# A state-space layer with a gated feed-forward branch: the gate product in bf16 pieces, the rank columns inside the steps' weights, the scan's masks built during the first steps

## What is computed

```python
x = L0_attn_hidden_states                       # (1, 1024, 512)
xn = _layernorm(x, axis=-1)
x = x + _L0_attn_ref(xn, ...) + _L0_ffn_ref(xn, ...)
```

```python
inter = xf @ c1_w.T @ c2_w.T                    # rank 16, 1792 units
blk = inter.reshape(B * T, n_blocks, SPARSITY)  # blocks of 32 units
idx = jnp.argmax(blk, axis=-1) + jnp.arange(0, INTER, SPARSITY)
h = jax.nn.relu(jnp.einsum('bkm,bm->bk', w1[idx], xf))
out = jnp.einsum('bk,bkm->bm', h, w2t[idx])
```

## Time and profile before

| | us |
|---|---|
| median of three runs | 1941.55 (1940.65 to 1942.32) |
| the profiled execution | 1946.74 |
| its span, first to last instruction | 1945.0 |
| mean granted clock of TensorE | 0.993 |
| prologue, up to the first inward product of the scan's tiles | 258.4 |

### The profile page before, as it was taken

One profiled execution on the slowest core, in us unless ns is written; L12 is line 12 of the kernel. 1 busy time (PEld: TensorE's weight loads), 2 busy tenths in 40 slices (PEclk: granted clock), 3 DMA queues, 4 the chain that ended last, 5 costly groups with the idle time before them and its releaser, 6 DMA issues.

```text
span 1945.0 us, 29309 instructions
## 1 busy us (share of the span) xinstructions
PE 1888.3 (97%) x10416; PEld 1478.3 (76%) x10416; DVE 1454.6 (75%) x1701; ACT 1169.6 (60%) x1908; POOL 951.2 (49%) x693
## 2 busy tenths in 40 slices
PE   7998999999999999999998999999999999999997
PEld 4776777777777777777776777878787878787875
DVE  6876645878787877778785878686878787877766
ACT  3334346767677776767676556566665656565643
POOL 6656643555555455555553444444344444444432
PEclk9999999999999999999999999999999999999998
DMA  2324463455454646464646353333424242424231
GB/s 88 119 82 141 137 218 93 134 164 181 148 188 135 210 131 225 136 213 128 208 131 222 86 153 128 114 110 95 146 77 155 83 161 82 156 77 150 77 115 44
DMA packets 123102, 264.62 MB, mean 136 GB/s; under 512 B 18112, under 2 KB 24384, under 8 KB 122704
## 3 DMA queue, kind: packets, MB, share of 16 engines
q1 hardware_dynamic: 88240, 161.55, 26.4%
q10 hardware_dynamic: 34720, 101.20, 16.2%
HBM read 216.82 MB, written 45.88 MB: 135 GB/s over the span
## 4 chain that ended last, share of the span: by engine, by line
PE 86%; issue 3%; POOL 3%; DVE 3%; DMA 3%; ACT 2%; ACTq 1%; SPq 0%; DVEq 0%; POOLq 0%
PE bank L1065 39%; PE bank L1123 6%; PE bank L1164 6%; PE bank L1185 5%; PE bank L1178 5%; PE bank L1098 5%; PE bank L1085 5%; PE bank L1130 3%; PE bank L721 3%; PE bank L694 3%; PE bank L1110 3%; PE bank L680 1%; DMA wlo_scratch<-stage 1%; POOL wxp L314 1%; DMA ecs<-ecs_scratch 1%
## 5 line engine op out<-in xcount | busy, mean ns | idle before, releaser
L1065 PE MATMUL bank<-xnp,wxp 128*128 128x512 f32 x3432 | 864.8, 404 | 11.3 <-POOL wxp L1443 6.4
L1065 PEld LDWEIGHTS bank<-xnp,wxp 128*128 128x128 f32 x3432 | 636.4, 189 | 164.0 <-POOL wxp L1443 16.6
L1443 POOL TENSOR_TENSOR wxp<-wxs,wxp 128x512 fp32r<-128x512 f32 x286 | 382.8, 1341 | 537.0 <-ACT wxp L1294 536.4
L1543 DVE SCALAR_TENSOR_TENSOR conv<-bank,cws,conv 128x509 f32<-128x509 f32 (+2 forms) x480 | 357.9, 746 | 11.3
L1301 ACT ACTIVATE conv<-bank,cbs,cws 128x512 f32<-128x512 f32 x160 | 124.2, 776 | 281.8 <-PE bank L1065 263.1
L1474 POOL TENSOR_TENSOR yl<-gT,yh 128x1024 fp32r<-128x1024 f32 x63 | 151.8, 2409 | 214.3 <-ACT yh L1359 214.3
L1294 ACT ACTIVATE wxp<-wxs 128x512 fp32r<-128x512 f32 x286 | 178.1, 623 | 0.7 <-DMA wxs<-wp 0.7
L1646 DVE SCALAR_TENSOR_TENSOR M<-M,gb 128x1024 f32<-128x1024 f32 x128 | 171.9, 1344 | 7.5 <-DVE gb L1638 0.5
L1345 ACT ACTIVATE ya<-xT,dch 128x128 f32<-128x128 f32 x512 | 156.1, 390 | 0.0
L1336 ACT ACTIVATE M<-bank 128x1024 f32<-128x1024 f32 x64 | 65.7, 1026 | 137.0 <-PE bank L1130 137.0
L1178 PE MATMUL bank<-wosh,yh 128*128 128x512 f32 x512 | 135.7, 407 | 5.1 <-issue 5.0
(11 more groups left out here) (166 smaller groups left out, 2847.0 us busy)
## 6 DMA issues: line engine op xcount, KB each, us to landing
wxs<-wp SPq DMA_DIRECT2D x288, 256.0 KB, 2.7
wosh<-whi_scratch ACTq DMA_DIRECT2D x64, 512.0 KB, 6.2
wosl<-wlo_scratch ACTq DMA_DIRECT2D x64, 512.0 KB, 11.2
ecs<-ecs_scratch ACTq DMA_DIRECT2D x112, 256.0 KB, 4.4
stage<-wout SPq DMA_DIRECT2D x64, 256.0 KB, 3.0
...
```

What stands on the lines that cost most here:

```text
L1065: last = pe.matmul(bank(k), wxp[:, k % 2, a, kk, :], xnp[:, b, kk, :], start=kk == 0 and a + b == 0, stop=kk == KT - 1 and a == 1)
L1443: pool.tensor_tensor(wxp[:, k % 2, 1], wxs[:, k % AHEAD], wxp[:, k % 2, 0], ALU.subtract).then_inc(w_lo, 1)
L1543: last = dve.scalar_tensor_tensor(out=conv[:, n % CB, back:], in0=bank(k)[:, 0:TH - back], scalar=cws[:, g, j, i:i + 1], in1=conv[:, n % C ...
```

## The change

**The gate product.** Ranks and c2 are each cut into three bf16 pieces that add up to the f32 value. Of the nine products of pieces the eight largest are kept, and the eight pairs stand side by side in the contraction: 8 slots of 16 rows make 128 rows. `tT` and `c2T` hold the pieces so, and `gate` is four bf16 matmuls with 128 rows. POOL cuts c2 (five operations), TensorE turns the 14 blocks (`turn_blocks`), ACT copies them (`blocks`). DVE cuts the ranks (`pack`, six operations per half), TensorE turns them (`turn_ranks`), ACT copies (`ranks`).

**The rank product.** c1's 16 columns are appended to the 128 of W_dt; `steps_of` computes both in 144 columns, and `to_rank` goes. `steps_of(0)` moves ahead of the flips of the second half; the DMA of its weights moves up in SyncE's queue.

**The masks.** Five of POOL's seven operations of the front and the three selects ahead of the loop move into turns 0 to 6 of the loop (`mask_part`), behind the turn's last `low`.

```diff
+SLOTS = P // RANK
...
-        c1s = sb(ctx, "c1s", [P, KT, RANK])
-        c2s = sb(ctx, "c2s", [RANK, INTER])
-        wdts = sb(ctx, "wdts", [P, KT, NH])
+        c2f = sb(ctx, "c2f", [P, FT, RANK])
+        c2p = sb(ctx, "c2p", [P, FT, SLOTS, RANK], BF16)
+        c2T = sb(ctx, "c2T", [P, FT, P], BF16)
+        wdts = sb(ctx, "wdts", [P, KT, NH + RANK])
...
-        tT = sb(ctx, "tT", [RANK, L])
+        rk = sb(ctx, "rk", [P, CH, RANK])
+        rkp = sb(ctx, "rkp", [P, CH, SLOTS, RANK], BF16)
+        tT = sb(ctx, "tT", [P, HALVES, TH], BF16)
...
+        early_blocks = gates.bitcast(BF16)
+        late_blocks = banks[0][:, TH:].bitcast(BF16)
+
+        def strips(half):
+            return banks[1 if half else 2].rearrange("p (c n) -> p c n", c=CH)
...
-            sp.dma_start(c1s[:], c1).then_inc(s_wc, 16)
-            sp.dma_start(c2s[:], c2).then_inc(s_wc, 16)
+            sp.dma_start(c2f[:], c2).then_inc(s_c2, 16)
+            sp.dma_start(wdts[:, :, 0:NH], wdt).then_inc(s_wc, 16)
+            sp.dma_start(wdts[:, :, NH:], c1).then_inc(s_wc, 16)
             sp.dma_start(wxs[:, 0], source(0)).then_inc(d_f[0], 16)
...
-            sp.dma_start(wdts[:], wdt).then_inc(s_wdt, 16)
...
-            pool.wait_ge(s_mask, 2)
-            pool.affine_select(out=segl[:], in_=segl[:], compare_op=ALU.is_ge, fill=0.0, base=0,
-                               pattern=[[0, 2], [0, CH], [1, P]], channel_multiplier=-2).then_inc(s_mask, 1)
...
-            pool.wait_ge(s_mask, 5)
...
+            pool.wait_ge(s_c2, 16)
+            three = c2f[:].unsqueeze(2).broadcast_to([P, FT, 3, RANK])
+            two = c2f[:].unsqueeze(2).broadcast_to([P, FT, 2, RANK])
+            pool.tensor_copy(c2p[:, :, 0::3], three).then_inc(s_cp, 1)
+            pool.wait_ge(s_cp, 1)
+            pool.tensor_tensor(c2f[:], c2f[:], c2p[:, :, 0], ALU.subtract).then_inc(s_cp, 1)
+            pool.wait_ge(s_cp, 2)
+            pool.tensor_copy(c2p[:, :, 1::3], three).then_inc(s_cp, 1)
+            pool.wait_ge(s_cp, 3)
+            pool.tensor_tensor(c2f[:], c2f[:], c2p[:, :, 1], ALU.subtract).then_inc(s_cp, 1)
+            pool.wait_ge(s_cp, 4)
+            pool.tensor_copy(c2p[:, :, 2::3], two).then_inc(s_cp, 1)
+            low(0)
             pool.wait_ge(s_part, 1)
             pool.tensor_tensor(xnp[:, 1], xnz[:], xnp[:, 0], ALU.subtract).then_inc(s_split, 1)
-            low(0)
             low(1)
...
-            for m in range(PARTS):
-                pool.wait_ge(s_mask, 5 + m)
...
+
+            def mask_part(n):
+
+                if n == 0:
+                    pool.wait_ge(s_mask, 2)
+                    pool.affine_select(out=segl[:], in_=segl[:], compare_op=ALU.is_ge, fill=0.0, base=0,
...
+                if n == 1:
+                    pool.affine_select(out=segr[:], in_=segr[:], compare_op=ALU.is_ge, fill=FAR, base=0,
...
+                if n == 2:
+                    pool.wait_ge(s_mask, 4)
+                    pool.affine_select(out=segl[:], in_=segl[:], compare_op=ALU.is_ge, fill=0.0, base=1,
...
+                if n == 3:
+                    pool.wait_ge(s_stage, 1)
+                    pool.wait_ge(s_lo, item1(n + 2) + 1)
+                    pool.memset(segr[PAIRS:], 0.0).then_inc(s_stage, 1)
+                    pool.wait_ge(s_stage, 2)
+                    pool.memset(segl[PAIRS:], 1.0).then_inc(s_mask, 1)
+                    pool.wait_ge(s_mask, 5)
+                if 4 <= n < 4 + PARTS:
+                    m = n - 4
+                    pool.wait_ge(s_mask, 5 + m)
+                    pool.affine_select(out=segr[:], in_=segr[:], compare_op=ALU.not_equal, fill=-1.0,
...
                 if n + 2 < STEPS:
                     low(item1(n + 2))
+                mask_part(n)
...
+                act.wait_ge(s_tt, half + 1)
+                act.activation(tT[:, half], spare.bitcast(BF16), ACT.Copy).then_inc(s_tc, 1)
...
             spread(0)
             for t in range(CH):
                 turned_x(t)
+            high(0)
+            part_x(0)
+            blocks(0)
             spread(1)
-            part_x(0)
+            blocks(1)
+            turned_x(4)
+            turned_x(5)
             ranks(0)
-            high(0)
-            for t in range(CH, NT):
-                turned_x(t)
+            turned_x(6)
+            turned_x(7)
+            high(1)
             part_x(1)
-            ranks(1)
-            high(1)
             copy_mask(0)
...
                 if n == 1:
                     act.wait_ge(s_sp, 2)
                     act.activation(tot[:], tot[:], ACT.Ln).then_inc(s_dact, 1)
+                if n == 1:
+                    ranks(1)
...
-                dve.tensor_tensor(v[:, half * CH:(half + 1) * CH, :],
-                                  banks[2][:, half * 512:(half + 1) * 512].rearrange("p (t h) -> p t h", t=CH),
+                dve.tensor_tensor(v[:, half * CH:(half + 1) * CH, :], strips(half)[:, :, 0:NH],
...
+            def pack(half):
+
+                dve.wait_ge(s_dtm, half + 1)
+                dve.tensor_copy(rk[:], strips(half)[:, :, NH:NH + RANK]).then_inc(s_tp, 1)
+                dve.wait_ge(s_tp, 6 * half + 1)
+                if half:
+                    dve.wait_ge(s_tt, half)
+                dve.tensor_copy(rkp[:, :, 0:3], rk[:].unsqueeze(2).broadcast_to([P, CH, 3, RANK])).then_inc(s_tp, 1)
+                dve.wait_ge(s_tp, 6 * half + 2)
+                dve.tensor_tensor(rk[:], rk[:], rkp[:, :, 0], ALU.subtract).then_inc(s_tp, 1)
+                dve.wait_ge(s_tp, 6 * half + 3)
+                dve.tensor_copy(rkp[:, :, 3:6], rk[:].unsqueeze(2).broadcast_to([P, CH, 3, RANK])).then_inc(s_tp, 1)
+                dve.wait_ge(s_tp, 6 * half + 4)
+                dve.tensor_tensor(rk[:], rk[:], rkp[:, :, 3], ALU.subtract).then_inc(s_tp, 1)
+                dve.wait_ge(s_tp, 6 * half + 5)
+                dve.tensor_copy(rkp[:, :, 6:8], rk[:].unsqueeze(2).broadcast_to([P, CH, 2, RANK])).then_inc(s_tp, 1)
...
-            for t in range(CH, NT):
-                normalize(t)
+            normalize(4)
+            normalize(5)
+            pack(0)
+            normalize(6)
+            normalize(7)
...
                     add_bias(1)
+                    pack(1)
...
@@ -675,9 +741,11 @@
                 half, f = n // FT, n % FT
                 if n:
                     pe.wait_ge(s_m, 4 * n - 2)
+                if f == 0:
+                    pe.wait_ge(s_tc, half + 1)
+                    pe.wait_ge(s_cc, 2)
                 for c in range(CH):
-                    t = half * CH + c
-                    last = pe.matmul(gates[:, c * P:(c + 1) * P], tT[:, t * P:(t + 1) * P], c2s[:, f * P:(f + 1) * P],
+                    last = pe.matmul(gates[:, c * P:(c + 1) * P], tT[:, half, c * P:(c + 1) * P], c2T[:, f, :],
...
+                if n == 3:
+                    pe.wait_ge(s_tc, 2)
...
-            def to_rank(half):
+            def steps_of(half):
                 pe.wait_ge(s_xnT, CH * (half + 1))
-                for k in range(KT):
-                    last = pe.matmul(banks[3][0:RANK, half * TH:(half + 1) * TH], c1s[:, k, :],
-                                     (xn1 if half else xnz)[:, k, :], start=k == 0, stop=k == KT - 1)
-                last.then_inc(s_r, 1)
-
...
-            def steps_of(half):
                 for c in range(CH):
-                    t = half * CH + c
                     for k in range(KT):
-                        last = pe.matmul(banks[2][:, t * P:(t + 1) * P], normed(t)[:, k, :], wdts[:, k, :],
+                        last = pe.matmul(strips(half)[:, c, 0:NH + RANK], normed(half * CH + c)[:, k, :], wdts[:, k, :],
...
+            def turn_blocks():
+                pe.wait_ge(s_const, 6)
+                pe.wait_ge(s_cp, 5)
+                for f in range(FT):
...
+                    last = pe.transpose(target, c2p[:, f].rearrange("p s r -> p (s r)"), identb[:])
+                    if f in (SLOTS - 1, FT - 1):
+                        last.then_inc(s_ct, 1)
...
+            def turn_ranks(half):
+                pe.wait_ge(s_tp, 6 * (half + 1))
+                for c in range(CH):
+                    last = pe.transpose(spare.bitcast(BF16)[:, c * P:(c + 1) * P],
+                                        rkp[:, c].rearrange("p s r -> p (s r)"), identb[:])
+                last.then_inc(s_tt, 1)
+
             for t in range(CH):
                 flip(t)
+            turn_blocks()
             pe.wait_ge(s_wc, 32)
-            to_rank(0)
+            steps_of(0)
             flip(4)
             flip(5)
-            pe.wait_ge(s_const, 6)
-            pe.wait_ge(s_rc, 1)
-            gate(0)
+            turn_ranks(0)
             flip(6)
             flip(7)
-            to_rank(1)
+            gate(0)
             inward(0)
             gate(1)
-            pe.wait_ge(s_rc, 2)
             turn(0)
-            pe.wait_ge(s_wdt, 48)
-            steps_of(0)
...
                     pe.wait_ge(s_v, 2)
```

(6 more changed lines are left out.)

39 lines of the change are left out of this document (19 added, 20 removed).

## The result

The changed kernel takes 1949.23 us (median of 11 runs, 1945.84 to 1951.59), the kernel before 1943.18 us in the same comparison (11 runs): ratio 1.0029, 95% interval 1.0021 to 1.0038. It is slower by some 6 us; 1925.5 was forecast. The profiled execution took 1948.32 us, span 1946.6, mean granted clock 0.988.

What follows compares the result with a forecast made beforehand. TensorE was taken as the prologue's bound, except the store loop in steps 13 to 19. Terms -7.2, -2.1, -3.4, -0.4 and -2.9 summed to -16.0 us: 1930.7, less 5.2 for the median, 1925.5; range 1919 to 1933.

Steps and rivals of the forecast that it cites:

- front: Prologue up to step 1: outward product 0 starts at 40.2 instead of 47.41 us, step 1 at 43.2; -7.2 us.
- steps 1 to 8: Shorter gates minus waits for POOL and mutual delay: -2.1 us, ends -6.9 and +1 (DVE's 7 us steps rule).
- rival C: Steps 13 to 19: idle gaps lower TensorE's clock; +3, 1928.5 us, chance 0.13; falls in all seven steps: 8.4, 1933.5.
- steps 20 to 27: Six gates give -5.2, but POOL's casts and subtractions of csT in steps 21 to 23 stand in the way; -2.9 us.
- rival E: All gates: a bf16 gate with 128 rows takes as long as before; -5.2, 1936.4 us; chance 0.05.
- DVE's five pick operations take 3.22 ... so the mask stands at 30.2: Front, after gate 0: the picks keep their profiled 3.22 us, so the mask is ready at 30.2 us.
- Eight gates: -6.9: Steps 1 to 8: each of eight gates saves 0.86 us where TensorE is the bound; -6.9 us.
- 11.5 + m: Steps 1 to 8: POOL's us for two steps with mask part m, against 2 x 6.33 for TensorE; excess +3.1 us.
- +0.8 for mutual delay: Steps 1 to 8: DVE and POOL delaying each other through the moved mask parts costs 0.8 us for all.
- A: Masks and picks fill POOL and DVE; steps 1 to 8 gain nothing; -11.9, 1929.6 us; chance 0.18.
- D: Steps 1 to 8: each mask part shuts DVE out twice, costing 25.8; +11.9 in all, 1953.5 us; chance 0.03.
- B: All gates count, the store loop of steps 13 to 19 shortening with them; -28.7, 1913 us; chance 0.06.

Runs made afterwards that it cites:

- splits_in_four: The change with each of the front's two POOL splits made in four operations of 512 columns; 0.9994 of the kernel before, outward product 0 at 41.4 us.
- masks_front: The change with the mask operations put back in the front, ahead of the steps; 0.9978 of the kernel before, steps 1 to 8 in 57.1 us.
- masks_late: The change with the mask parts in steps 8 to 14 instead of 0 to 6; 0.9995 of the kernel before, steps 9 to 12 in 31.2 us.
- memset_parts: The change with the mask parts' six selects replaced by memsets, which read nothing; 1.0010 of the kernel before, steps 1 to 8 in 62.6 us.
- stores_apart: The change with one piece of wout in every second step; 1.0000 of the kernel before, steps 13 to 19 in 58.5 us.

## Why the prediction was wrong

By its own terms, from the starts of step 1, 9, 13 and 20:

| term | forecast | measured | what it was |
|---|---|---|---|
| front | -7.2 | -0.5 | one mask product held up for 4.5 us, and the clock |
| steps 1 to 8 | -2.1 | +8.1 | gates -2.2 instead of -6.9; masks +10.3 instead of about +3.9 |
| steps 9 to 12 | -3.4 | -4.0 | as forecast |
| steps 13 to 19 | -0.4 | +2.2 | rival C |
| steps 20 to 27 | -2.9 | -0.2 | waits for POOL, as feared, and one fall of the clock |
| sum | -16.0 | +5.6 | |

**The gate product** was right: 0.22 forecast, 0.21 measured. So rival E falls.

**The front's chain** had TensorE's and DVE's links and left out POOL. Its first half came out by luck: gate 0 started at 27.05 for 26.8, but the steps' product had ended at 21.0 and not at 23.9, and DVE's normalizations, held up beside the first split, kept the rank pieces waiting until 23.20. The step that failed is "DVE's five pick operations take 3.22 ... so the mask stands at 30.2". It took the duration of an operation from a place where POOL was idle or short, and put it to a time at which the sum itself had moved POOL's longest operation. The rule was quoted one paragraph on, for the masks alone. `splits_in_four` shows that up to 5.6 of the missing 6.7 us were the two splits, most of it this one product and the clock behind it.

**Steps 1 to 8, first half of the error**: "Eight gates: -6.9". `masks_front` measured 2.2. DVE's 7 us a step were read, and even set down as the end "+1" of the range, but the sum went by TensorE and let 6.33 us per step stand under a DVE that needs about 7 (57.1 us for eight steps in `masks_front`). It also put `pack(1)` at nothing, which in `masks_front` stands ahead of step 1's hidden units.

**Second half**: "11.5 + m" and "+0.8 for mutual delay". `masks_late` shows the rule's form holds where DVE has room, without the clock. `memset_parts` shows the mutual delay at about 3.7 us with its clock fall, not 0.8. The falls of the clock, 4.6 us of the masks' 10.3, had no term at all in this stage. The remainder is POOL's plain time on a loop that DVE already filled: by the chain, POOL had to hand over at once what DVE gave it late, and a part in its way was seen.

**The rivals.** A said that nothing would be gained in steps 1 to 8; D that masks would cost DVE two blocks a part, +25.8. The sign was D's. D's mechanism, mutual exclusion, is about 3.7 us of D's 25.8; the rest of the loss is POOL's plain time and the clock, and POOL and not DVE ends the waits. The marker was right: over 59 us in this stage, A or D. D's chance of 0.03 was too small for a mechanism that a rule and a row both spoke for. In C's side case 1925.5 and 8.4 make 1933.9 and not 1933.5. C was right in kind: two falls in steps 13 to 19 (184.12 and 196.00) instead of one, three in steps 1 to 8 where it was not looked for. B is contradicted: in steps 13 to 19 nothing of the gates came through, and `stores_apart` shows why, the loop being 6.6 us of it and a wait with the exponentials in it next.

**The chances.** 0.93 for faster rested on adding up five gains as if each lay with TensorE. In steps 1 to 8 DVE was busy 89% of the time before, and 12% off TensorE's step put it behind DVE; the five stages' errors also had one cause, POOL and DVE, and were taken as independent.
